# Linear attention stage of an adaLN block: the turn of a finished chunk behind the next unit's products on TensorE

## The chip, the cores and the metric

The kernel runs on one core of a Trainium2 chip. The metric is the device time of one execution in microseconds. Before the change the median of three runs is 692.49 us (689.46 to 693.12).

## What is computed

The reference is one block with adaptive layer norms over `x` of 8 batches, 512 tokens and 128 features: a causal linear attention, then a softmax attention and a mixture of experts. The part around the change is the linear attention:

```python
q = (jax.nn.elu(q) + 1.0 + FEAT_EPS) / jnp.sqrt(E)          # 16 heads of 8
k = jax.nn.elu(k) + 1.0 + FEAT_EPS
kv_cumsum = jnp.cumsum(jnp.einsum('blhe,blhf->blhef', k, v), axis=1)
k_cumsum = jnp.cumsum(k, axis=1)
num = jnp.einsum('blhe,blhef->blhf', q, kv_cumsum)
den = jnp.einsum('blhe,blhe->blh', q, k_cumsum)[..., None] + FEAT_EPS
out = (num / den).reshape(B, L, D) @ Wout.T + bout
```

Around it, in the same block: `x = x + ga * layernorm(out)`, `h = layernorm(x) * (1 + cb) + sb`, then queries, keys and values of the softmax attention from `h`, softmax attention over 512 tokens in 16 heads, and an expert per token (8 experts, 128 to 512 to 128, gelu).

## The kernel before, in words

The kernel is written engine by engine: each engine has its own program, and semaphores tie them together. In the linear stage all of them walk the same double loop, steps `s` from -3 to 8 (a pass for each batch) and in each `d` from 0 to 7. Unit `g = 8 s + d` is half of a chunk of 128 tokens of batch `s`: 8 of the 16 heads. A chunk `q` is two units.

What happens to a unit and a chunk:

- `products(g)` (TensorE, L912 to L925): eight matmuls of keys by queries into two banks, `b_at`. It waits until VectorE has masked unit g - 1 (`s_am`), since there is one pair of banks.
- `masked(g)` (VectorE, L1405 to L1410): two multiplications with the causal mask (L1409) from these banks into SBUF. It waits for the products (`s_at`) and for the numerators of unit g - 2 (`s_nm`).
- `numerators(g)` (TensorE, L927 to L940): sixteen recorded matmuls (L936) of masked products by values into bank `b_nm`. It waits for the mask and, in the first unit of a chunk, until ScalarE has copied the numerators of the chunk before.
- `numerators_out(q)` (ScalarE, L1956 to L1959): that copy, into `nt`.
- `turn(q)` (TensorE, L942 to L956): four transposes of `nt` (L946) and, for all chunks of a batch but the first, a matmul of the queries by the state of the earlier chunks (L952), into bank `b_tr`. It waits for the copy.
- `denominators(q)` and `normalise(q)` (VectorE, L1424 and L1429) divide. `turn_back(q)` (L961), `output_out(q)` (ScalarE, L1963), `project(q)` (L967) and `output(q)` (VectorE, L1437) make the output rows, and `squares(q)` (ScalarE, L2011) its squares.

Beside the units, the same steps carry the work of three other batches: the projections and features of batch s + 2 (`a_...`: L983, L990, L995, L1005, L1012 on TensorE; L1568, L1573, L1579, L1583 on VectorE; L1977, L1985, L1990, L1997, L2001, L2005 on ScalarE), the state of batch s + 1 (L975, masked by L1416), and layer norms and softmax projections of batches s - 2 and s - 3 (`c_...`: L1021, L1026, L1033, L1040 on TensorE; L1441, L1448, L1450, L1589 on VectorE; L2018, L2027, L2042, L2046 on ScalarE; L656 to L687 on POOL, where `h_ready` is L681 and L683). SP stores the features of a batch to DRAM (L208) and reads them back as stacks in twelve DMAs (L221).

The order on TensorE around the change, in an even step `d` (L1268 to L1316): `turn_back` of an earlier chunk; a projection, transposes or the state where that step has one; `turn` of the chunk whose second unit is g - 1; `products(g + 1)`; `numerators(g)`. Each engine takes its instructions in its program's order.

Behind the linear stage come the softmax attention (row maxima L1051 and L1596, scores L1079, exponentials L2058, values L1090) and the experts (L1338, L1347).

Of the kernel before, what the change touches and what calls it, by code (L numbers as in the profile page):

```python
# [199 lines left out]
def wait(eng, sem, value):  # L200

    if isinstance(value, int) and value <= 0:
        return
    eng.wait_ge(sem, value)
# [46 lines left out]
def program(nc, k):  # L251
# [21 lines left out]
    with ExitStack() as ctx, ExitStack() as early:  # L273
# [101 lines left out]
        def has(b):  # L375
            return 0 <= b < B

        def chunk(q):
            return 0 <= q < B * C

        def unit(g):
            return 0 <= g < B * NL
# [116 lines left out]
        with nc.Block() as block:  # L499
# [411 lines left out]
            def _(pe):  # L911
                def products(g):  # L912
                    b, d = g // NL, g % NL
                    c, hp, u = d // 2, d % 2, b % 2
                    if d == 0:
                        pe.wait_ge(k.s_stk[u], (b // 2 + 1) * N_STACK)
                    wait(pe, s_am, 2 * g)
                    for j in range(GH):
                        for gg in range(2):
                            p = GH * (2 * hp + gg) + j  # L920
                            rows = slice(HALF * LIN_HALF[p], HALF * LIN_HALF[p] + KR)
                            last = pe.matmul(b_at[gg][:, j * P:(j + 1) * P],  # L922
                                             ks[u][rows, LIN_SLOT[p], c * P:(c + 1) * P],
                                             qs[u][rows, LIN_SLOT[p], c * P:(c + 1) * P], start=True, stop=True)
                    last.then_inc(s_at, 1)  # L925
# [32 lines left out]
                def turn_back(q):  # L958
                    pe.wait_ge(s_on, q + 1)
                    wait(pe, s_yc, q)  # L960
                    pe.transpose(b_oy[:, 0:P], on[:, q % 2, :], k.ident).then_inc(s_ot, 1)  # L961

                def project(q):
                    if q == 0:
                        pe.wait_ge(w_s_v, SETUP)
                    pe.wait_ge(s_oc, q + 1)
                    pe.matmul(b_oy[:, 0:P], ot[:, q % 2, :], k.woutt[:], start=True, stop=True).then_inc(s_y, 1)  # L967

                def state(b):
                    pe.wait_ge(s_vp, b + 1)  # L970
                    pe.wait_ge(a_s_kc, b + 1)
                    wait(pe, c_s_r1, 2 * (b - 4) + 2)
                    for c in range(C - 1):
                        for i in range(c + 1):
                            last = pe.matmul(b_z[:, c * H * (E + 1):(c + 1) * H * (E + 1)], tile(k.h_all, b, i),  # L975
                                             vp[b % 2][:, i], start=(i == 0), stop=(i == c))
                    last.then_inc(s_sm, 1)

                def a_turn(a):
                    pe.wait_ge(a_s_xn, a + 1)  # L980
                    wait(pe, c_s_r1, 2 * (a - 5) + 1)
                    for c in range(C):
                        last = pe.transpose(b_x[:, c * P:(c + 1) * P], a_xn[:, c * D:(c + 1) * D], k.ident)  # L983
                    last.then_inc(a_s_tr, 1)

                def a_query(a):
                    pe.wait_ge(a_s_ht, a + 1)
                    if a == 0:
                        pe.wait_ge(w_s_v, QUERY)
                    pe.matmul(b_x[:], k.wlt[:, 0:D], a_ht[:], start=True, stop=True).then_inc(a_s_pj, 1)  # L990

                def a_key(a):
                    wait(pe, a_s_kc, a)
                    wait(pe, c_s_vc, a - 4)
                    pe.matmul(b_y[:], k.wlt[:, D:2 * D], a_ht[:], start=True, stop=True).then_inc(a_s_pj, 1)  # L995
# [13 lines left out]
                def a_key_turn(a):  # L1009
                    pe.wait_ge(a_s_ph, 2 * a + 2)  # L1010
                    for c in range(C):
                        last = pe.transpose(b_y[:, c * P:(c + 1) * P], a_fk[:, c * P:(c + 1) * P], k.ident)  # L1012
                    last.then_inc(a_s_kt, 1)
# [10 lines left out]
                def c_query(b):  # L1024
                    pe.wait_ge(c_s_ht, b + 1)
                    pe.matmul(b_x[:], k.wsm[:, 0:D], c_ht[:], start=True, stop=True).then_inc(c_s_pj, 1)  # L1026

                def c_key(b):
                    if has(b + 4):
                        pe.wait_ge(a_s_vc, b + 5)  # L1030
                    pe.wait_ge(s_sp, min(b + 4, B))
                    wait(pe, c_s_r1, 2 * b)
                    pe.matmul(b_z[:], k.wsm[:, D:2 * D], c_ht[:], start=True, stop=True).then_inc(c_s_pj, 1)  # L1033

                def c_value(b):
                    if has(b + 4):
                        pe.wait_ge(a_s_kc, b + 5)
                    wait(pe, c_s_vc, b)
                    for c in range(C):
                        last = pe.matmul(b_y[:, c * P:(c + 1) * P], c_ht[:, c * P:(c + 1) * P], k.wsm[:, 2 * D:3 * D],  # L1040
                                         start=True, stop=True)
                    last.then_inc(c_s_v, 1)
# [225 lines left out]
                for s in STEPS:  # L1268
                    for d in range(NL):
                        g = s * NL + d  # L1270
                        if s == -2 and d == 2:
                            pe.wait_ge(w_s_b, 16 * 5)
                            pe.transpose(k.bank[4][:, 0:P], wl_raw[:, 2, :], k.ident).then_inc(w_s_t, 1)
                        if s == -2 and d == 5:
                            pe.matmul(k.bank[3][0:B, :], ct, wm[:, 2 * D:NM * D], start=True, stop=True
                                      ).then_inc(w_s_m, 1)
                        if s == -1 and d == 5:
                            pe.wait_ge(w_s_v, WO)
                            pe.wait_ge(w_s_ct, 1)
                            pe.matmul(k.bank[4][:, P:2 * P], wo_pos, center, start=True, stop=True).then_inc(w_s_t, 1)  # L1280
                        if s == -1 and d == NL - 1:
                            pe.wait_ge(w_s_mr, 5)
                            pe.wait_ge(s_init, 1)
                        if d % 2 == 0 and chunk((g - 4) // 2):
                            turn_back((g - 4) // 2)
                        if d % 2 == 1 and chunk((g - 5) // 2):
                            project((g - 5) // 2)
                        if d == 0 and has(s - 3):
                            c_key(s - 3)
                        if d == 1 and has(s - 3):  # L1290
                            c_value(s - 3)
                        if d == 1 and has(s + 2):
                            a_turn(s + 2)
                        if d == 2 and has(s + 1) and s != -1:
                            state(s + 1)
                        if d == 3 and has(s + 2):
                            a_query(s + 2)
                            a_key(s + 2)
                        if d == 4 and has(s + 2):
                            a_value(s + 2)  # L1300
                        if d == 5 and has(s - 2):
                            c_turn(s - 2)
                        if d == 7 and has(s + 2) and s != -1:
                            a_key_turn(s + 2)
                        if s == 0 and d == 0:
                            pe.wait_ge(a_s_vc, 2)
                            state(0)
                            a_key_turn(1)
                        if d == 7 and has(s - 2) and s < B:
                            c_query(s - 2)  # L1310
                        if d % 2 == 0 and chunk((g - 2) // 2):
                            turn((g - 2) // 2)
                        if unit(g + 1):
                            products(g + 1)
                        if unit(g):
                            numerators(g)  # L1316
                        if s == B:
                            for m in range(4 * d, 4 * d + 4):
                                early_maximum(m)
                            if d == 4:  # L1320
                                pe.wait_ge(s_nt, B * C)
                                turn_maxima(0, b_num)
# [957 lines left out]
```

## Time and profile before

| | |
|---|---|
| median of three runs | 692.49 us |
| lowest, highest | 689.46, 693.12 us |
| the profiled execution | 689.38 us |
| its span in the profile | 687.6 us |
| TensorE, VectorE, ScalarE, POOL busy | 89%, 86%, 73%, 60% |
| linear stage with products of units | 29 to 215 us |

The profile is of one execution. The span is the time from the first to the last recorded instruction, and the execution's own time holds 1.8 us more around it. A row of the timeline has its start, its length, the engine, the line, what is written and read, and in brackets how long the engine waited before it and who released it. The granted clock of TensorE is given as a share of 2.4 GHz.

### The profile page before, as it was taken

The numbers are of one execution on the slowest core, as the hardware profiler recorded it, in microseconds if no ns is written. First come the engines' busy times: TensorE is split into PE (matmuls) and PEld (weight loads), VectorE is DVE, ScalarE is ACT, GpSimd is POOL, SyncE is SP. The second block draws the span as 40 slices with busy tenths as digits, with TensorE's granted clock in tenths as the row PEclk, the third lists the DMA queues.
The fourth block names the chain that finished last, engine by engine and source line by source line (L and its number), as shares of the span: only waits on it lengthen the run. The fifth ranks groups of instructions, "written<-read, shape, count | busy, mean of one in ns | idle before, by whom it ended". The sixth has DMA issues, their size and how long they took to land.

```text
span 687.6 us, 16368 instructions
## 1 busy us (share of the span) xinstructions
PE 610.6 (89%) x5305; PEld 304.8 (44%) x5305; DVE 590.7 (86%) x1489; ACT 500.5 (73%) x1071; POOL 411.6 (60%) x922
## 2 busy tenths in 40 slices
PE   4689789988877788999999999999999999899994
PEld 2456456655544222222333332333323322589993
DVE  6878999998877988899999999999999994775552
ACT  3545677787655387888888888888888889765661
POOL 4213558667656642436676887877877862566553
PEclk9899999999999699999999999999999999999997
DMA  6564234335364121137110301203012010556510
GB/s 181 161 229 131 66 107 135 120 116 185 113 165 139 48 92 47 47 107 231 49 47 2 116 25 53 77 13 116 25 52 78 13 48 23 139 174 174 167 33 9
DMA packets 42899, 66.25 MB, mean 96 GB/s; under 512 B 7948, under 2 KB 36335, under 8 KB 39808
## 3 DMA queue, kind: packets, MB, share of 16 engines
q1 hardware_dynamic: 39232, 56.73, 27.9%
q0 software_dynamic: 3296, 8.41, 3.4%
q8 instruction: 44, 0.72, 0.4%
q14 instruction: 39, 0.32, 0.2%
q10 hardware_dynamic: 288, 0.07, 0.0%
HBM read 41.64 MB, written 22.26 MB: 93 GB/s over the span
## 4 chain that ended last, share of the span: by engine, by line
PE 53%; ACT 18%; DVE 16%; issue 6%; SPq 2%; POOL 2%; DMA 2%; ACTq 0%; POOLq 0%; DVEq 0%
PE bank L1090 12%; ACT arena L2058 11%; PE pair L1079 8%; PE bank L1051 7%; PE pair L1338 4%; DVE arena L1409 4%; DVE arena L1596 3%; PE bank L1101 2%; PE bank L1347 2%; PE pair L1347 2%; PE bank L936 2%; PE pair L1131 2%; DVE fq_all L1573 1%; PE pair L990 1%; PE pair L1051 1%
## 5 line engine op out<-in xcount | busy, mean ns | idle before, releaser
L2058 ACT ACTIVATE arena<-pair 128x512 f32<-128x512 f32 x506 | 278.1, 602 | 52.8 <-PE pair L1079 50.9
L1596 DVE TENSOR_REDUCE arena<-bank 128x1 f32<-128x512 f32 x388 | 251.3, 682 | 10.1 <-PE bank L1051 7.2
L1079 PE MATMUL pair<-q_stack,k_stack 64*128 64x512 bf16 x506 | 158.7, 388 | 5.4 <-ACT arena L2058 4.9
L1051 PE MATMUL bank<-k_stack,q_stack 63*128 63x512 bf16 x388 | 136.0, 394 | 10.3 <-DVE arena L1596 6.0
L1090 PE MATMUL bank<-arena,values 128*9 128x512 f32 x1024 | 134.7, 598 | 1.6 <-ACT arena L2058 1.5
L1409 DVE TENSOR_TENSOR arena<-bank,cst 128x512 f32<-128x512 f32 x128 | 82.0, 681 | 12.8 <-PE bank L922 12.5
L1596 DVE TENSOR_REDUCE arena<-pair 128x1 f32<-128x512 f32 x124 | 84.3, 680 | 2.7 <-PE pair L1051 2.3
L726 POOL TENSOR_TENSOR arena<-arena 128x32 f32<-128x32 f32 (+6 forms) x312 | 68.4, 219 | 24.4
L1051 PEld LDWEIGHTS bank<-k_stack,q_stack 63*128 63x128 bf16 x388 | 33.1, 93 | 110.5 <-ACT arena L2063 25.9
L1079 PEld LDWEIGHTS pair<-q_stack,k_stack 64*128 64x128 bf16 x506 | 40.7, 93 | 47.4 <-ACT arena L2058 23.2
L1051 PE MATMUL pair<-k_stack,q_stack 63*128 63x512 bf16 x124 | 48.8, 393 | 0.7 <-ACT v_all L2083 0.3
L1959 ACT ACTIVATE arena<-bank,den_eps 128x512 f32<-128x512 f32 x32 | 21.8, 680 | 33.9 <-PE bank L936 33.9
L890 POOL DMA_INDIRECT out_dram<-arena,e_token_u x32 | 31.2, 975 | 23.1 <-DVE arena L1904 19.6
L762 POOL DMA_INDIRECT token_rows<-arena,d_places_u x32 | 33.6, 1050 | 15.4 <-POOL d_places_u L750 5.0
L2196 ACT ACTIVATE fq_all<-pair 128x512 f32<-128x512 f32 x39 | 23.3, 596 | 26.3 <-PE pair L1338 26.3
L1338 PE MATMUL pair<-q_stack,h_all 128*128 128x128 f32 x312 | 41.5, 276 | 0.0
L936 PE MATMUL bank<-arena,values 128*9 128x128 f32 x1024 | 40.4, 276 | 0.0
L649 POOL TENSOR_TENSOR arena<-arena 128x512 bf16<-128x512 f32 x15 | 17.4, 1161 | 35.5 <-ACT arena L2001 35.5
L1338 PEld LDWEIGHTS pair<-q_stack,h_all 128*128 128x128 f32 x312 | 38.0, 192 | 0.0
L922 PE MATMUL bank<-q_stack,k_stack 63*128 63x128 bf16 x512 | 25.6, 220 | 12.3 <-DVE arena L1409 11.2
L1090 PEld LDWEIGHTS bank<-arena,values 128*9 128x9 f32 x1024 | 15.2, 88 | 40.8 <-issue 29.9
L946 PE MATMUL bank<-cst,arena 128*128 128x128 f32 x128 | 20.4, 282 | 9.9 <-ACT arena L1959 9.7
(307 smaller groups left out, 1211.9 us busy)
## 6 DMA issues: line engine op xcount, KB each, us to landing
softmax_parts<-arena SPq DMA_DIRECT2D x8, 768.0 KB
q_stack<-softmax_parts SPq DMA_DIRECT2D x48, 128.0 KB
k_stack<-softmax_parts SPq DMA_DIRECT2D x48, 128.0 KB
linear_parts<-arena SPq DMA_DIRECT2D x7, 768.0 KB, 3.7
q_stack<-linear_parts SPq DMA_DIRECT2D x42, 128.0 KB
k_stack<-linear_parts SPq DMA_DIRECT2D x42, 128.0 KB
arena<-in_L_ffn_w_dram SPq DMA_DIRECT2D x16, 256.0 KB, 5.0
v_all<-token_rows SPq DMA_DIRECT2D x20, 192.5 KB, 2.7
```

Source lines behind the costliest of these rows:

```text
L726: done(pool.tensor_tensor(half[:, 0:w], src[:, 0:w], src[:, w:2 * w], ALU.add))
L762: pool.indirect_dma_start(k.rows_dram, bass.IndirectOffsetOnAxis(ap=k.pos_u[:, f:f + 1], axis=0), row_slot(f), None, bounds_check=NE * REG ...
L890: pool.indirect_dma_start(out_rows, bass.IndirectOffsetOnAxis(ap=token_u[:, j:j + 1], axis=0), yo[j], None, bounds_check=T * P - 1, oob_is ...
L936: last = pe.matmul(b_nm[VW * j:VW * j + E + 1, cols], vp[u][:, c, GH * (2 * hp + gg) + j, :], b_am[:, g % 2, gg, j, :], start=True, stop=T ...
L1051: pe.matmul(bank[:], qs[b % 2][rows, slot, qt * P:(qt + 1) * P], ks[b % 2][rows, slot, :], start=True, stop=True).then_inc(d_s_m, 1)
L1079: pe.matmul(score_bank(s)[:], ks[u][rows, 2 * g + x, kt * P:(kt + 1) * P], qs[u][rows, 2 * g + x, :], start=True, stop=True).then_inc(d_s_ ...
L1090: last = pe.matmul(b_num[VW * q:VW * q + E + 1, :], vp[b % 2][:, kt, GH * g + q, :], pt[:, kt % 2, q % 2, q // 2, :], start=(kt == 0), sto ...
L1338: last = pe.matmul(b_up[j % 2][:, c * P:(c + 1) * P], w1c[j % R4][:, c * P:(c + 1) * P], xt[j % R4], start=True, stop=True)
L1347: last = pe.matmul(b_dn[j % 2][:, 0:D], hid[j % R4][:, c * P:(c + 1) * P], k.w2_all[:, bass.ds(e * HID + c * D, D)], start=(c == 0), stop= ...
L1409: dve.tensor_tensor(b_am[:, g % 2, gg], k.tiles(b_at[gg][:], GH), k.rep(k.causal, GH), ALU.mult).then_inc(s_am, 1)
L1596: dve.reduce_max(mx[:, m % 2, col:col + 1], bank[:], AX).then_inc(d_s_mr, 1)
L2058: act.activation(pt[:, kt % 2, x, half, :], score_bank(s)[:], ACT.Exp, scale=SCALE).then_inc(d_s_e, 1)
```

## The change

In every even step the call of `turn` moves behind `products(g + 1)` and stands ahead of `numerators(g)`.

```diff
                         if d == 7 and has(s - 2) and s < B:
                             c_query(s - 2)
+                        if unit(g + 1):
+                            products(g + 1)
                         if d % 2 == 0 and chunk((g - 2) // 2):
                             turn((g - 2) // 2)
-                        if unit(g + 1):
-                            products(g + 1)
                         if unit(g):
                             numerators(g)
```

TensorE's program, pass s = 3, step 6 and the first half of step 7; behind each row are the semaphores that it waits for. Before:

```order
L961 MATMUL pair<-cst,arena 128x128 [waits b_projected_out,b_normalised]
L946 MATMUL bank<-cst,arena 128x128 [waits b_normalised,b_numerators_out]
L946 MATMUL bank<-cst,arena 128x128 x3
L952 MATMUL bank<-arena,fq_all 128x16x9
L922 MATMUL bank<-q_stack,k_stack 128x128 [waits b_masked]
L922 MATMUL bank<-q_stack,k_stack 128x128 x7
L936 MATMUL bank<-arena,values 9x128 [waits b_masked,b_numerators_out]
L936 MATMUL bank<-arena,values 9x128 x7
L967 MATMUL pair<-woutt,arena 128x128 [waits b_output_copied]
L1012 MATMUL pair<-cst,arena 128x128 [waits a_features]
L1012 MATMUL pair<-cst,arena 128x128 x3
L1026 MATMUL pair<-arena,wsm 128x512 [waits c_h_transposed]
```

After:

```order
L961 MATMUL pair<-cst,arena 128x128 [waits b_projected_out,b_normalised]
L922 MATMUL bank<-q_stack,k_stack 128x128 [waits b_masked]
L922 MATMUL bank<-q_stack,k_stack 128x128 x7
L946 MATMUL bank<-cst,arena 128x128 [waits b_normalised,b_numerators_out]
L946 MATMUL bank<-cst,arena 128x128 x3
L952 MATMUL bank<-arena,fq_all 128x16x9
L936 MATMUL bank<-arena,values 9x128 [waits b_masked,b_numerators_out]
L936 MATMUL bank<-arena,values 9x128 x7
L967 MATMUL pair<-woutt,arena 128x128 [waits b_output_copied]
L1012 MATMUL pair<-cst,arena 128x128 [waits a_features]
L1012 MATMUL pair<-cst,arena 128x128 x3
L1026 MATMUL pair<-arena,wsm 128x512 [waits c_h_transposed]
```

The five matmuls of the turn (L946, L952) now stand between the products (L922), which wait for the mask, and the numerators (L936).

The same engine in pass s = 7, step 2, where there is no projection beside the units, as one piece of the difference:

```order
 L961 MATMUL pair<-cst,arena 128x128
-L946 MATMUL bank<-cst,arena 128x128 x4
-L922 MATMUL bank<-q_stack,k_stack 128x128 x8
-L936 MATMUL bank<-arena,values 9x128 x8
-L967 MATMUL pair<-woutt,arena 128x128
-L922 MATMUL bank<-q_stack,k_stack 128x128 x8
-L936 MATMUL bank<-arena,values 9x128 x8
-L961 MATMUL pair<-cst,arena 128x128
-L946 MATMUL bank<-cst,arena 128x128 x4
```

This is the turn of a batch's first chunk: four transposes and no L952. In the difference it goes behind the first eight L922, and the next one, in step 4, goes behind the eight L922 that follow it. The orders of VectorE, ScalarE, POOL and SP are the same before and after.

## Rows read from the trace of the kernel before

**Rows 1.** The page, busy times; granted clock in 40 slices of 17.2 us.

```profile
PE 610.6 (89%) x5305; PEld 304.8 (44%) x5305; DVE 590.7 (86%) x1489; ACT 500.5 (73%) x1071; POOL 411.6 (60%) x922
...
PEclk9899999999999699999999999999999999999997
```

**Rows 2.** Stretches, whole core: length, busy us of each engine, clock, DMA.

```profile
110.00:134.00 24.00, 21.31 (x279) 14.31 (x276) 22.74 (x71) 18.55 (x49) 16.61 (x22) 1.00 0.43 133
...
182.00:222.00 40.00, 30.16 (x406) 18.75 (x405) 30.61 (x99) 22.50 (x62) 24.33 (x30) 1.00 0.56 159
```

**Rows 3.** Waits, 30 to 225 us: who waited for whom, us, times, longest.

```profile
DVE arena L1409 <- PE bank L922: 12.5, 15, 1.6
...
PE bank L922 <- DVE arena L1409: 11.2, 14, 2.0
...
PE bank L946 <- ACT arena L1959: 9.7, 16, 1.3
```

**Rows 4.** Timeline of TensorE, steps 6, 7 and 0 of a steady pass.

```profile
95.42 0.65 PE L946 MATMUL bank<-cst,arena 128*128 128x128 f32 x4 [0.55 <-ACT arena L1959]
...
97.33 0.40 PE L922 MATMUL bank<-q_stack,k_stack 63*128 63x128 bf16 x8 [1.01 <-DVE arena L1409]
...
97.66 0.62 PE L936 MATMUL bank<-arena,values 128*9 128x128 f32 x16
...
99.93 0.40 PE L922 MATMUL bank<-q_stack,k_stack 63*128 63x128 bf16 x8
...
102.27 0.65 PE L946 MATMUL bank<-cst,arena 128*128 128x128 f32 x4 [0.27 <-ACT arena L1959]
...
103.43 0.63 PE L936 MATMUL bank<-arena,values 128*9 128x128 f32 x16
```

**Rows 5.** Timeline of VectorE, the mask of the next pass.

```profile
100.86 1.27 DVE L1409 TENSOR_TENSOR arena<-bank,cst 128x512 f32<-128x512 f32 x2
```

**Rows 6.** Timeline of TensorE, ScalarE and VectorE, steps 2 to 4.

```profile
106.79 1.64 PE L975 MATMUL pair<-values,h_all 128*128 128x144 f32 x12
...
108.49 0.66 PE L946 MATMUL bank<-cst,arena 128*128 128x128 f32 x4
...
113.12 0.69 ACT L1959 ACTIVATE arena<-bank,den_eps 128x512 f32<-128x512 f32 x1 [2.56 <-PE bank L936]
...
114.88 0.75 DVE L1568 TENSOR_SCALAR fq_all<-pair,bq 128x512 f32<-128x512 f32 x1 [1.05 <-ACT arena L1990]
```

**Rows 7.** Timeline of VectorE and TensorE, passes 1 and 2 of the stage.

```profile
55.40 1.27 DVE L1409 TENSOR_TENSOR arena<-bank,cst 128x512 f32<-128x512 f32 x2
...
56.28 0.66 PE L946 MATMUL bank<-cst,arena 128*128 128x128 f32 x4 [0.55 <-ACT arena L1959]
...
71.52 0.66 PE L946 MATMUL bank<-cst,arena 128*128 128x128 f32 x4 [0.55 <-ACT arena L1959]
...
74.40 0.40 PE L922 MATMUL bank<-q_stack,k_stack 63*128 63x128 bf16 x8 [1.98 <-DVE arena L1409]
```

**Rows 8.** Timeline of ScalarE, behind the last store of the chain.

```profile
195.45 0.60 ACT L2042 ACTIVATE arena<-pair 128x512 bf16<-128x512 f32 x1 [4.16 <-DMA softmax_parts<-arena]
```

**Rows 9.** Timeline of POOL, VectorE and TensorE, the stage's last pass.

```profile
202.05 1.28 POOL L683 TENSOR_TENSOR h_all<-arena 128x512 f32<-128x512 f32 x1
...
202.79 1.29 DVE L1409 TENSOR_TENSOR arena<-bank,cst 128x512 f32<-128x512 f32 x2 [1.25 <-PE bank L922]
...
211.74 0.66 PE L946 MATMUL bank<-cst,arena 128*128 128x128 f32 x4 [0.88 <-ACT arena L1959]
```

**Rows 10.** Clock of one stretch; TensorE around two falls.

```profile
35.00:40.00 5.00, 4.85 (x43) 3.79 (x44) 3.17 (x14) 2.97 (x6) 2.43 (x4) 0.66 0.82 330
...
35.15 0.97 PE L983 MATMUL pair<-cst,arena 128*128 128x128 f32 x4 [1.84 <-ACT arena L1977]
...
36.05 0.61 PE L922 MATMUL bank<-q_stack,k_stack 63*128 63x128 bf16 x8
...
228.14 1.21 PE L1051 MATMUL bank<-k_stack,q_stack 63*128 63x512 bf16 x2 [1.80 <-DVE arena L1596]
```

## The prediction

> **What bounds the kernel now.** The page's busy shares [rows 1] name no single engine: TensorE 89%, VectorE 86%. So I went to the stage that the change touches, the linear stage, and read it by stretches [rows 2]: in a steady pass of 24 us VectorE is busy for 22.74 us and TensorE for 21.31, at full clock; in the last passes of the stage (182 to 222 us) VectorE is busy for only 30.61 of 40 us. The list of waits of the stage [rows 3] shows both sides of the exchange that is edited: the turn (L946) waits for ScalarE's copy of the numerators (L1959), 9.7 us in 16 waits; the products (L922) wait for VectorE's mask (L1409), 11.2 us in 14; and the mask waits for the products, 12.5 us in 15. (The PEld rows are weight loads of the same waits, and are not added.)
>
> **What the change does to one even step.** 31 turns are moved; the last one has no products behind it. Each even unit g has three ready times: P, when TensorE has ended what stands ahead; A, when ScalarE has copied the numerators (the turn needs it); M, when VectorE has masked unit g (the products of g+1 need it, since they overwrite the banks that were masked). The turn takes 0.84 us with its second matmul after a wait (0.78 when TensorE comes busy, 0.6 for the first chunk of a batch, which has no second matmul), the products take 0.33 (together 102.27 to 103.43 [rows 4]).
> Before: products at max(max(P, A) + 0.84, M), numerators 0.33 later.
> After: products at max(P, M), numerators at max(products + 0.33, A) + 0.84.
> So where the copy (A) comes last, the products win up to 0.84 us plus the wait and the numerators up to 0.33; where the mask (M) comes last, the turn no longer fills that wait, and the numerators and all behind them on TensorE lose up to 0.84. No instruction, semaphore or DMA is added; the orders of the other engines and of SP are the same. The consumer of the turn, VectorE's reciprocal (L1424), stands behind the mask of g+1, whose 1.28 us begin about 0.44 after the products; the turn is done by then, so its own delay costs nothing.
>
> **Steady pass, step 6 (M last).** Before, TensorE waited 0.55 us for A, the turn ran at 95.42 and the products waited for the mask until 97.33 [rows 4]. After, products still at 97.33, then the turn, numerators at 98.44 in place of 97.66: +0.78. Step 7 is dense (L967, L1012, L1026 back to back), so the products for unit 0 of the next pass go from 99.93 to 100.71, and their mask from 100.86 [rows 5] to 100.71 + 0.44 = 101.15: **+0.29**. In step 0 A (102.27) no longer costs anything, so TensorE is 0.39 late behind it. In step 2 L975 starts at 106.79 and takes about 1.47 to the next matmul, so P = 108.26, and A = 108.49 [rows 6]; before, numerators at 108.49 + 0.59 + 0.33 = 109.41; after, P = 108.65, A = 108.78 (it hangs on VectorE, +0.29), numerators at 109.54: +0.13. From there the chain runs over L990, L995 and the numerators of step 3 to ScalarE, which has waited 2.56 us for them [rows 6], and by the exp to VectorE's L1568, which has waited 1.05 us [rows 6]. VectorE's own 0.2 or 0.3 is absorbed in that 1.05, so a steady pass costs **+0.13**. The pattern stands in three passes (steps 2 at 108, 132 and 156 us): +0.39.
>
> **The first passes.** In the first, at 56.28, the turn waited for A, but M is 55.40 + 1.28 + 0.06 = 56.74 [rows 7]: after, numerators at 56.74 + 0.33 + 0.84 = 57.91 against 57.45, of which I keep **+0.42** (the turn comes without its wait) down to the exp of that pass. In the pass behind it the turn (71.52) stood inside the wait for M that ends at 74.40 [rows 7]; its 0.84 lands ahead of another wait for the mask, in step 7, so that pass and the next cost about 0.
>
> **The end of the stage.** The slip reaches the store of the last batch's parts. From there the chain is transfers and SP's issues until ScalarE goes on at 195.45, after 4.16 us of waiting for a store [rows 8]; TensorE's order doesn't matter in between. The store hangs on VectorE's step 0 and 1, +0.29. So 0.42 + 0.39 + 0.29 = **+1.1** arrive at 195.45. Behind it the change pays: VectorE waited 1.25 us, to 202.79, for products that stood behind a turn that waited for A [rows 9]. After, this mask starts at 201.6; the statistics behind it need POOL's h_all, which ends at 202.05 + 1.28 = 203.33, so they gain 0.76 of the 1.2. Over POOL's power chain and ScalarE this comes to the turn of 211.74 [rows 9], where A is now 210.98. M is the mask that is 0.7 earlier too (210.73), so the products go at 210.73, the turn at 211.06 and the numerators at 211.87 (0.03 of lag), in place of 211.74 + 0.84 + 0.33 = 212.91: **-1.03**, carried by L1026 and the last turn to VectorE's maxima. Sum of the plain terms: +1.1 - 1.03 = **+0.1 us**. Each term is uncertain by a few tenths (semaphore lags of 0.04 to 0.07), the sum by about 1.
>
> **The clock.** What the sum leaves out is that waits are no longer broken up. In a steady pass TensorE waited 0.55 us ahead of 95.42 and 1.01 ahead of 97.33 [rows 4]; after, it waits from 94.87 to 97.33, 2.5 us in one piece, in four passes; in the pass before from 70.97 to 74.40, 3.4 us in place of 0.55 and 1.98 [rows 7]. The granted clock shows what such waits did in this run [rows 10]: with 1.84 us of waiting ahead of 35.15 it fell from 2.4 to 1.2 GHz, and so it did with the 1.80 ahead of 228.14, behind a stretch with many short waits (the slice of 223 to 241 us has a mean between six and seven tenths [rows 1]); the 1.98 us ahead of 74.40 [rows 7], with the turn shortly before, did not bring it down (all slices from 52 to 223 us show 9 [rows 1]). So the cases lie near each other, and 2.5 or 3.4 us unbroken are beyond any that passed. Price of one fall: the stretch 35 to 40 us has a mean clock of 0.66 [rows 10], which is 3.4 of its 5 us at half speed; eight products that start at 36.05 took 0.61 there, first start to last end, against 0.40 at full clock, where the next group starts 0.33 behind (0.54 there), so 3.4 x (1 - 0.33/0.54) = 1.3 us of TensorE's work is lost, on a stretch (steps 7 and 0) whose 0.49 us of slack the 0.78 has already used. Bounds: 0 falls, 0 us; five falls, 6.6 us. I take two, nearest to what the mixed rows say: **+2.6**. The Trainium skill's page "TensorE: Matmul & The Clock Gate", section "HAM oscillation — how this bites in real kernels", says that a kernel whose matmuls wait in every round can fall back to the lower clock in every round. By that rule alone it would be all five. Our rows have waits on both sides, so it is a rival below and not the sum.
>
> Sum: +0.1 + 2.6 = +2.7 us against the profiled execution (689.38, span 687.6). The same on the median, 692.49, which lies 3.1 above that execution: **695.2 us**. A measurement of this kernel can tell about 0.5%, 3.5 us, from no change.
>
> **Rivals.**
> 1. The clock holds in all passes: +0.1, **692.6**. For it: 1.98 us ahead of 74.40 passed. Against: 1.80 and 1.84 did not.
> 2. It falls in all five waits, once in each: 5 x 1.3 + 0.1 = +6.6, **699.1**. For it: each wait is longer than any that passed. Against: with waits of 1.80 to 1.98 us the rows show both outcomes, so length alone does not decide.
> 3. Faster: the slips are swallowed (VectorE's idle 1.05 and the SP chain) and only the end gains, -1.0; and, since the stage ends denser, the low clock behind 223 us [rows 1] stays out. Rows 1 have about 0.35 of 17.2 us, 6 us, lost by the clock there, of which I take 2.3 on the chain (the rest lies beside VectorE's maxima): -3.3, **689.2**. The point from which it decides is whether TensorE waits less than now ahead of 228.14; that wait is for VectorE's statistics, which the change does not touch. Little speaks for it.
> 4. The turn is so late that VectorE's reciprocal waits for it, as at half clock (turn about 1.4 us, mask 1.28): some 0.3 in each of the 31 steps at worst, 9 us, but only at half clock; it widens rival 2, to about 700.
>
> **Chances.** Forecast (one to three falls, 694 to 697.5) 0.46, clock holds 0.24, all five or more 0.20, faster end 0.10. Of the forecast a bit over half lies within 0.5% (below 695.95): same 0.26 + 0.24 + 0.03 = 0.53; slower 0.20 + 0.20 = 0.40; faster than 689.03 by rival 3: 0.07. The range leaves out the ends of rivals 2, 3 and 4: 690.5 to 699.5.
>
> **What would show it.** In the changed kernel's profile: one wait of about 2.5 us ahead of the products in step 6 of each steady pass and none left ahead of the turn; VectorE's wait of 1.25 us ahead of the mask at 202.79 gone; granted clock below 1.00 in one to three slices between 70 and 180 us. No fall there, and the forecast's 2.6 is wrong. If the turn still waits for ScalarE in most steps, the reading of who comes last is wrong. If the stage ends earlier than before by more than 1 us at full clock, the steady slips are not on the chain.

## The result and the profile after

The changed kernel takes 702.72 us in the median of four runs (700.01 to 704.02) against 692.50 before (689.46 to 693.12): ratio 1.0149, 95% interval 1.0121 to 1.0177, or 10.2 us more. The forecast was 695.2, the range ended at 699.5. The profiled execution took 703.78 us, its span 702.0. The two profiled executions lie further apart than the medians, by 14.40 us: that of before, 689.38, is 3.1 us below its median, that of the changed kernel 1.1 above. Sums read from the traces answer to the 14.40, the ratio to the 10.2.

The page of the changed kernel, to be laid beside [rows 1] (a slice is now 17.55 us):

```profile
PE 627.8 (89%) x5305; PEld 315.9 (45%) x5305; DVE 592.0 (84%) x1489; ACT 501.8 (71%) x1071; POOL 411.5 (59%) x922
...
PEclk9888999889899769999999999999999999999998
```

VectorE, ScalarE and POOL have what they had; TensorE has 17.2 us more busy time for the same 5305 matmuls, and where [rows 1] has nines from 52 to 223 us, there are now four eights from 52 to 194 us (a slice with 3.4 us at half clock still has a mean of 0.90 and prints as a nine). The same stretches as [rows 2]:

```profile
110.00:134.00 24.00, 20.88 (x242) 14.23 (x243) 19.86 (x58) 16.14 (x40) 16.38 (x20) 0.86 0.43 133
...
182.00:222.00 40.00, 34.12 (x432) 21.91 (x431) 30.54 (x98) 22.41 (x60) 21.23 (x25) 0.89 0.44 120
```

In 110 to 134 us VectorE, the busiest engine there before (22.74 us in 71 instructions), does 19.86 in 58, at a mean clock of 0.86: less work gets through in the same 24 us. The waits that answer to [rows 3], for 30 to 235 us:

```profile
PE bank L922 <- DVE arena L1409: 21.8, 16, 3.4
...
PE bank L946 <- ACT arena L1959: 1.2, 2, 1.0
```

The turn hardly waits for ScalarE any more (1.2 us for 9.7), and the products wait twice as long for the mask (21.8 for 11.2). The change did what it says: it moved the wait and made one piece of two. TensorE around step 6 of the pass that [rows 4] show:

```profile
98.40 0.33 PE L961 MATMUL pair<-cst,arena 128*128 128x128 f32 x1
101.18 0.40 PE L922 MATMUL bank<-q_stack,k_stack 63*128 63x128 bf16 x8 [2.46 <-DVE arena L1409]
101.51 0.73 PE L946 MATMUL bank<-cst,arena 128*128 128x128 f32 x4
102.03 0.69 PE L952 MATMUL bank<-arena,fq_all 128*128 128x144 f32 x2
102.65 1.04 PE L936 MATMUL bank<-arena,values 128*9 128x128 f32 x16
...
127.03 0.61 PE L922 MATMUL bank<-q_stack,k_stack 63*128 63x128 bf16 x8 [2.47 <-DVE arena L1409]
...
153.90 0.61 PE L922 MATMUL bank<-q_stack,k_stack 63*128 63x128 bf16 x8 [2.46 <-DVE arena L1409]
...
180.99 0.61 PE L922 MATMUL bank<-q_stack,k_stack 63*128 63x128 bf16 x8 [2.47 <-DVE arena L1409]
```

One wait of 2.46 us, and behind it the L952 take 0.69 us and the sixteen L936 1.04, in place of 0.41 and 0.62. Stretches of it (length, busy us of each engine, clock):

```profile
102.00:105.40 3.40, 3.40 (x27) 2.60 (x26) 2.63 (x7) 2.62 (x7) 1.16 (x1) 0.50 0.00 0
105.50:109.00 3.50, 3.50 (x41) 1.64 (x40) 2.42 (x8) 2.80 (x8) 0.00 (x0) 1.00 0.00 0
125.90:132.70 6.80, 5.67 (x38) 3.82 (x38) 4.72 (x10) 4.17 (x9) 2.17 (x2) 0.50 0.36 128
...
153.20:160.00 6.80, 6.10 (x38) 3.82 (x38) 4.30 (x10) 3.75 (x8) 1.73 (x2) 0.50 0.19 66
```

0.50 is 1.2 GHz, 1.00 is 2.4 GHz: 3.4 us at the lower level behind the first of these waits, 6.8 us each behind the next two. In the trace every one of the six passes 0 to 5 has such a stretch at its step 6: 50.8 to 57.6, 78.1 to 81.5, 102.0 to 105.4, 125.9 to 132.7, 153.2 to 160.0 and 180.5 to 187.3 us, and 201.0 to 204.4 another: 37.5 us in all, where the kernel before has none between 38.7 and 226.5. VectorE then waits for TensorE's next products:

```profile
106.62 1.29 DVE L1409 TENSOR_TENSOR arena<-bank,cst 128x512 f32<-128x512 f32 x2 [1.08 <-PE bank L922]
```

The products of step 6 start later than before by 0.69 us in pass 0 (52.51 against 51.82), by 2.93 in pass 1 (77.33 against 74.40), then by 3.85 (101.18 against 97.33), 5.77 (127.03 against 121.26), 8.72 and 11.90, and the first maxima of the softmax stage (L1051) by 14.62 (231.72 against 217.10). The whole execution is 14.40 longer. So all of it arises in the linear stage, pass by pass.

### The profile page after: what moved, and what is told of

The parts are those of the page before. It is cut to its first block, busy times and chain, and to the rows that moved or that the text cites. A ratio compares the mean times of both kernels' runs of the same rounds, so it can differ in the third digit from the quotient of the medians.

```text
span 702.0 us, 16368 instructions
## 1 busy us (share of the span) xinstructions
PE 627.8 (89%) x5305; PEld 315.9 (45%) x5305; DVE 592.0 (84%) x1489; ACT 501.8 (71%) x1071; POOL 411.5 (59%) x922
## 4 chain that ended last, share of the span: by engine, by line
PE 63%; ACT 16%; DVE 10%; issue 4%; SPq 2%; DMA 2%; POOL 1%; ACTq 0%; POOLq 0%; DVEq 0%
PE bank L1090 12%; ACT arena L2058 11%; PE pair L1079 7%; PE bank L1051 7%; PE pair L1338 5%; PE bank L936 3%; DVE arena L1596 3%; DVE arena L1409 3%; PE pair L1347 3%; PE bank L1347 3%; PE bank L1101 2%; PE bank L922 2%; PE bank L946 2%; PE pair L975 2%; PE pair L1131 1%
## 5 line engine op out<-in xcount | busy, mean ns | idle before, releaser
L1051 PE MATMUL bank<-k_stack,q_stack 63*128 63x512 bf16 x388 | 136.5, 396 | 8.8 <-DVE arena L1596 4.8
L1409 DVE TENSOR_TENSOR arena<-bank,cst 128x512 f32<-128x512 f32 x128 | 82.0, 682 | 15.0 <-PE bank L922 14.8
L1051 PEld LDWEIGHTS bank<-k_stack,q_stack 63*128 63x128 bf16 x388 | 33.1, 93 | 110.0 <-ACT arena L2063 24.8
L1051 PE MATMUL pair<-k_stack,q_stack 63*128 63x512 bf16 x124 | 49.0, 395 | 0.6 <-ACT v_all L2083 0.3
L1959 ACT ACTIVATE arena<-bank,den_eps 128x512 f32<-128x512 f32 x32 | 21.8, 682 | 36.0 <-PE bank L936 35.9
L922 PE MATMUL bank<-q_stack,k_stack 63*128 63x128 bf16 x512 | 27.0, 229 | 21.8 <-DVE arena L1409 21.8
L936 PE MATMUL bank<-arena,values 128*9 128x128 f32 x1024 | 42.9, 289 | 0.0
L922 PEld LDWEIGHTS bank<-q_stack,k_stack 63*128 63x128 bf16 x512 | 15.4, 99 | 44.4 <-DVE arena L1409 29.2
L660 POOL TENSOR_SCALAR arena<-arena 128x4 f32<-128x4 f32 x16 | 3.7, 229 | 53.2 <-DVE arena L1450 53.2
```

The source lines that it names most:

```text
L922: last = pe.matmul(b_at[gg][:, j * P:(j + 1) * P], ks[u][rows, LIN_SLOT[p], c * P:(c + 1) * P], qs[u][rows, LIN_SLOT[p], c * P:(c + 1) * P ...
L936: last = pe.matmul(b_nm[VW * j:VW * j + E + 1, cols], vp[u][:, c, GH * (2 * hp + gg) + j, :], b_am[:, g % 2, gg, j, :], start=True, stop=T ...
L1051: pe.matmul(bank[:], qs[b % 2][rows, slot, qt * P:(qt + 1) * P], ks[b % 2][rows, slot, :], start=True, stop=True).then_inc(d_s_m, 1)
L1409: dve.tensor_tensor(b_am[:, g % 2, gg], k.tiles(b_at[gg][:], GH), k.rep(k.causal, GH), ALU.mult).then_inc(s_am, 1)
```

## The experiments

**Theory.** The wait in one piece of step 6 brings the clock down in every pass, and that is the loss. **First rival:** the order itself costs it (numerators and all behind them late, the turn late), and the lower clock only goes along with it. **Second rival:** the loss comes from the turns moved in the other steps. The kernels ran on other chips, in three groups (1 to 4; 5, 6, 9 and 10; 7, 8, 11 and 12), each with runs of the kernel before (medians 706.89, 706.37 and 706.02 us there), and are told by their ratio to it; 1% is 7.1 us. Times in the expectations of 1 to 4 are those of the first chip, so only their ratios can be compared. No trace of the kernel before was taken on those chips. Those chips need some 14 us more for the kernel before. It lies behind the linear stage (in experiment 1 L1051 starts 2.62 us later than in the trace of before, and the execution ends 17.0 later) and was not followed up. Times of the trace are compared with the trace of before shown above. Lines behind an edit are numbered a few higher in these kernels (L1409 is L1412 or L1415 there, L975 is L976).

**1. The wait filled.** Changed order, but in step 6 of passes 0 to 5 the turn is also issued ahead of the products, without its signal; the real one, behind, writes the same over it. So the order that counts is the changed one, with 0.84 us of matmuls in the wait.

```diff
+                        if d == 6 and 0 <= s < 6:
+                            turn((g - 2) // 2, False)
                         if unit(g + 1):
                             products(g + 1)
```

> The changed order; in step 6 of passes 0 to 5 the five matmuls of the turn are also issued ahead of the products (their result is written over by the real turn behind the products, so nothing is left out). TensorE's wait for the mask is broken up as before, and the delay of 0.78 us of the numerators stays. Clock theory (the fall to 1.2 GHz behind the unbroken wait costs the time): no low clock between 45 and 210 us, time 691 to 694 us, 9 to 11 us under the changed kernel. Rival, the order itself (each pass's numerators, ScalarE and POOL come later): 700 to 703 us, with the clock at 2.4 GHz.

Measured: 706.98 us, ratio 1.0011 (0.9994 to 1.0028). The lower clock is left at 75.5 to 79.0 and 123.3 to 126.7 us, 6.8 us in all. With five more matmuls per pass nearly all of the loss is gone, so the order by itself isn't what costs 1.5%: the first rival falls as the explanation. What the order does cost is measured in 5. The expectation of no lower clock at all was missed by two passes of six.

**2. One step put back.** Changed order, but in step 6 up to pass 5 the turn stands ahead again.

```diff
+                        ahead = d == 6 and s < 6
+                        if chunk_ready and ahead:
+                            turn((g - 2) // 2)
                         if unit(g + 1):
                             products(g + 1)
-                        if chunk_ready:
+                        if chunk_ready and not ahead:
                             turn((g - 2) // 2)
```

(`chunk_ready` stands for `d % 2 == 0 and chunk((g - 2) // 2)`. The next experiments have the same form, and only `ahead` is shown.)

> The changed order, but in step 6 of passes up to 5 the turn stands ahead of the products again; 25 of 31 turns stay moved. Clock theory: no low clock in the steady passes, and the gain at the end of the stage (about 1.9 us between unit 56 and unit 63 in the changed kernel's trace) stays: 690 to 691.5 us. Rival, each moved turn costs a little: about 10.2 x 25/31 = 8 us over the kernel before, 700 us.

Measured: 705.24 us, ratio 0.9976 (0.9955 to 0.9998). The turns moved elsewhere cost nothing in sum: the second rival falls. But the trace is not free of the lower clock, as it was expected to be: it has 17.1 us of it, at 54.9 to 58.3, 75.3 to 78.7, 123.1 to 126.5, 188.0 to 191.4 and 208.5 to 211.9 us. The third of these lies in a steady pass, behind a wait that was broken up:

```profile
122.33 0.40 PE L922 MATMUL bank<-q_stack,k_stack 63*128 63x128 bf16 x8 [1.12 <-DVE arena L1412]
```

```profile
123.10:126.50 3.40, 3.40 (x16) 1.78 (x8) 2.83 (x7) 3.06 (x7) 1.16 (x1) 0.50 0.11 33
```

**3. That step alone.** The order of before, moved in step 6 of passes 0 to 5 alone, six turns of 31.

```diff
+                        ahead = not (d == 6 and 0 <= s < 6)
```

> The kernel before, with the turn moved only in step 6 of passes 0 to 5 (6 of 31). Clock theory: all of the loss and none of the gain at the end: 10.2 + 1.9 = 12 us over the kernel before, 703 to 706 us, with a low clock in each of the six passes. Rival, each moved turn costs a little: 10.2 x 6/31 = 2 us, 694.5 us.

Measured: 718.33 us, ratio 1.0158 (1.0141 to 1.0175), 34.1 us of lower clock between 45 and 225 us, L1051 at 231.12. Two of its waits:

```profile
100.69 0.40 PE L922 MATMUL bank<-q_stack,k_stack 63*128 63x128 bf16 x8 [2.46 <-DVE arena L1412]
...
126.54 0.61 PE L922 MATMUL bank<-q_stack,k_stack 63*128 63x128 bf16 x8 [2.46 <-DVE arena L1412]
```

The six turns give the whole loss, and the second wait shows the products (0.61 us) already at the lower clock.

**4. The last passes alone.** The order of before, moved in passes 6 to 8 alone.

```diff
+                        ahead = s < 6
```

> The kernel before, with the turn moved only in passes 6 to 8. If the gain of the stage's end is the products that no longer stand behind a turn that waits for ScalarE: 1 to 2 us faster than before, 690.5 to 691.5 us, first maxima (L1051) 1 to 2 us earlier, clock as before up to 222 us. Rival, in the changed kernel the end only caught up because its chain of stores had slack: no difference, 692.5 us.

Measured: 706.06 us, ratio 0.9981 (0.9960 to 1.0002). The interval reaches 1, so a gain is not shown, and its trace has none: in the last passes the clock falls at 188.4 to 191.8 and 208.9 to 212.3 us, which was not expected, and the kernel is 2.41 us behind the trace of before at step 6 of pass 5 and 2.96 behind at L1051. The second of these falls begins with step 4 of pass 7, where the mask comes last and the turn no longer stands ahead of the products:

```profile
207.74 0.30 PE L961 MATMUL pair<-cst,arena 128*128 128x128 f32 x1 [0.98 <-DVE v_all L1440]
208.84 0.61 PE L922 MATMUL bank<-q_stack,k_stack 63*128 63x128 bf16 x8 [0.81 <-DVE arena L1412]
```

Of the seven traces with this order in step 4 of the last passes (the changed kernel's two, 1, 2, 4, 6, 7), five have such a fall between 188 and 225 us (all but 1 and 7), 3.4 to 6.8 us in all; the three that keep the turn ahead there (9, 11, 12) have none up to 223 us.

**5. That step, with the wait filled.** As 3, with the copy of 1: the price of the order without most of the clock's.

```diff
+                        if d == 6 and 0 <= s < 6:
+                            turn((g - 2) // 2, False)
+                        ahead = not (d == 6 and 0 <= s < 6)
```

> Turn moved only in step 6 of passes 0 to 5, and there its five matmuls are also issued ahead of the products (written over by the real turn): the delay of the numerators by itself, at full clock, without the gain of the other turns. By the sum of the prediction +1.1 us over the kernel before (ratio 1.0016); by the offsets of the run in which the turn is issued twice (+0.37 in a pass without low clock) 6 x 0.37 = +2.2 us, ratio 1.003. Rival, the delay costs its whole 0.78 in every pass: +4.7 us, ratio 1.007.

Measured: 709.61 us, ratio 1.0039 (1.0015 to 1.0064), 2.8 us. TensorE in step 6:

```profile
122.18 0.66 PE L946 MATMUL bank<-cst,arena 128*128 128x128 f32 x4 [0.55 <-ACT arena L1965]
122.68 0.41 PE L952 MATMUL bank<-arena,fq_all 128*128 128x144 f32 x2
124.10 0.40 PE L922 MATMUL bank<-q_stack,k_stack 63*128 63x128 bf16 x8 [1.01 <-DVE arena L1415]
124.42 0.66 PE L946 MATMUL bank<-cst,arena 128*128 128x128 f32 x4
```

Its products of step 6 come at 99.80, 124.10, 148.40 and 172.69 us, that is 2.47, 2.84, 3.22 and 3.60 behind those of before: 0.37 a pass at full clock. Falls of 3.4 us are left in passes 0 and 1 (52.2 and 76.1 us).

3 and 5 have the same order and differ in the copy alone: 1.0158 against 1.0039. This pair weighs most for the theory.

**6. Less in the wait.** Changed order, with only one matmul of the turn (a transpose) in the wait of step 6, at the same place as the copy of 1.

```diff
+                        if d == 6 and 0 <= s < 6:
+                            pe.wait_ge(s_nt, (g - 2) // 2 + 1)
+                            wait(pe, s_on, (g - 2) // 2)
+                            pe.matmul(b_tr[:, 0:P], nt[:, (g - 2) // 2 % 2, 0:P], k.ident, start=True, stop=True,
+                                      is_transpose=True, skip_group_check=True)
```

> The changed kernel, with one matmul of the turn (of five, 0.27 us) issued in the wait of step 6 of passes 0 to 5 (written over later). If any break in the wait holds the clock: as with the whole turn, ratio 1.001. If it is the amount of work in the wait: the clock still falls in most passes, ratio 1.010 to 1.015. Rival of no clock effect at all: 1.015.

Measured: 713.36 us, ratio 1.0086 (1.0057 to 1.0115), 20.5 us of lower clock. It stands in the trace (the transpose takes 0.33 us, not the 0.27 expected) as

```profile
124.33 0.33 PE L1314 MATMUL bank<-cst,arena 128*128 128x128 f32 x1 [0.55 <-ACT arena L1964]
126.24 0.40 PE L922 MATMUL bank<-q_stack,k_stack 63*128 63x128 bf16 x8 [1.58 <-DVE arena L1414]
```

and 1.58 us unbroken behind it. This pass holds. Of the six step-6 waits four still have a fall behind them, of 3.4 us each (13.7 us; the rest of the 20.5 lies in the last passes): less filling, less gain. So neither of the two clear-cut expectations came true; 1.0086 lies between them.

**7. The same work elsewhere.** A control for 1: changed order, the copy in step 4 in place of step 6.

```diff
+                        if d == 4 and 0 <= s < 6:
+                            turn((g - 2) // 2, False)
```

> Control: the changed kernel, the second copy of the turn's five matmuls put into step 4 of passes 0 to 5, where TensorE has no wait ahead of the products, in place of step 6 (written over as before). Clock theory: the wait of 2.5 us in step 6 is whole, the clock falls as in the changed kernel: ratio 1.013 to 1.018. Rival, any additional work of TensorE in a pass holds the clock: ratio 1.001 as with the copy in step 6.

**8. The changed kernel, once more,** in the same group as 7.

> The changed kernel again, on the chip of these runs: ratio 1.012 to 1.018 as before if the loss is that of the kernel and not of the first chip.

Measured: the control 714.28 us, ratio 1.0106 (1.0066 to 1.0146), 30.7 us of lower clock; the changed kernel 716.98 us, ratio 1.0135 (1.0094 to 1.0177), 41.0 us. A step 6 of the control, then a stretch around two step 6 there:

```profile
100.69 0.40 PE L922 MATMUL bank<-q_stack,k_stack 63*128 63x128 bf16 x8 [2.46 <-DVE arena L1412]
101.02 0.66 PE L946 MATMUL bank<-cst,arena 128*128 128x128 f32 x4
101.52 0.42 PE L952 MATMUL bank<-arena,fq_all 128*128 128x144 f32 x2
101.86 1.04 PE L936 MATMUL bank<-arena,values 128*9 128x128 f32 x16
```

```profile
98.00:106.00 8.00, 5.54 (x47) 3.40 (x47) 6.29 (x12) 5.89 (x14) 3.58 (x3) 0.79 0.21 68
122.00:132.00 10.00, 7.54 (x69) 5.05 (x69) 8.07 (x17) 7.10 (x18) 5.24 (x5) 0.68 0.47 143
```

The same stretches of 5, with the same order in step 6 and the wait filled:

```profile
98.00:106.00 8.00, 6.99 (x81) 4.56 (x83) 7.72 (x18) 6.96 (x19) 2.70 (x3) 1.00 0.17 44
122.00:132.00 10.00, 8.81 (x109) 6.05 (x110) 9.69 (x26) 8.18 (x21) 3.77 (x5) 1.00 0.26 91
```

The copy in step 4 leaves the wait of 2.46 us and the falls behind it; most of the loss stays. The control came out below what was expected of it, but its interval overlaps that of the changed kernel, so whether it helps at all is not settled.

The executions of one kernel, whose order is the same in all, say the same. Time and mean granted clock of the fastest and the slowest: the control 707.92 us at 0.955 and 716.37 at 0.941, experiment 6 706.65 at 0.961 and 714.88 at 0.946, the changed kernel 712.18 at 0.952 and 719.15 at 0.939. That is 7 to 8.5 us for some 20 us more at half clock, 0.36 to 0.41 us for each.

**9 to 12. Looking for a better order.** First (9) the order that the traces suggest: the turn ahead where the mask comes last (step 6 up to pass 5, step 4 of the last passes), behind elsewhere, and the copy in the step 6 named.

```diff
+                        if d == 6 and 0 <= s < 6:
+                            turn((g - 2) // 2, False)
+                        ahead = (d == 6 and s < 6) or (d == 4 and s >= 6)
```

> Turn ahead of the products where the mask comes last (step 6 of passes up to 5, step 4 of passes 6 and 7), behind them elsewhere; in step 6 of passes 0 to 5 it is issued twice, both ahead of the products. If the low clock in the kernel before's own waits (a wait of 1.98 us in pass 1) costs something, the second copy takes it away: ratio 0.994 to 0.996, 3 to 4 us. If the second copy does nothing, the ratio is that of the run with step 6 ahead, 0.9976.

Measured: 704.87 us, ratio 0.9988 (0.9964 to 1.0012): no gain is shown; the interval holds the 0.9976 expected if the copy did nothing, and not the 0.994 to 0.996. Then (10) the order of before with the turn twice in step 6 of passes 0 to 5, both ahead of the products (`ahead = True`, and the copy as above):

> The kernel before, with the turn issued twice in step 6 of passes 0 to 5, both ahead of the products (no order changed). If the clock of the kernel before also falls in some executions in these waits (it did in two profiled runs of this series, at 55 to 62 and 75 to 79 us): 1 to 2 us faster, ratio 0.997 to 0.9985. Rival, TensorE is on the path there and 0.8 us more work costs: ratio 1.002 or more.

Measured: 704.34 us, ratio 0.9975 (0.9957 to 0.9994). Then (11) both gains: this order and copy up to pass 5, and from pass 6 the turn behind the products but in step 4.

```diff
+                        if d == 6 and 0 <= s < 6:
+                            turn((g - 2) // 2, False)
+                        ahead = s < 6 or d == 4
```

> Both parts that were faster: the order of the kernel before up to pass 5 with the turn issued twice in step 6, and the turn behind the products in passes 6 to 8 but for step 4, where the mask comes last. If the two gains add up (0.9975 and 0.9981): ratio 0.9955 to 0.996, 3 us. If both are the same executions' gain: 0.9975.

Measured: 702.46 us, ratio 0.9963 (0.9942 to 0.9984), the lowest of these medians and between the two cases of the expectation. The page's clock line and one of the filled waits:

```profile
PEclk9899999999998599999999999999999999978998
```

```profile
96.20 0.60 PE L946 MATMUL bank<-cst,arena 128*128 128x128 f32 x4
96.64 0.41 PE L952 MATMUL bank<-arena,fq_all 128*128 128x144 f32 x2
97.38 0.40 PE L922 MATMUL bank<-q_stack,k_stack 63*128 63x128 bf16 x8 [0.33 <-DVE arena L1415]
```

Its stage runs to pass 5 as before does (97.38 for 97.33), and L1051 starts at 215.96, 1.14 earlier. Last (12), with a third turn in the wait of passes 0 and 1 (`for copy in range(2 if s < 2 else 1)` around the copy):

> As the run before it, and in passes 0 and 1, whose waits are longest (0.89 and 1.98 us behind the turn), the turn is issued three times. If the low clock that the runs still show near 55 and 75 us costs 1 to 2 us: ratio 0.993 to 0.995. If TensorE's slack there is already used: ratio 0.996 to 0.998.

Measured: 703.32 us, ratio 0.9960 (0.9943 to 0.9977), which the interval doesn't tell from the one before it.

## Why the prediction was wrong, and where right

**Who comes last: right.** The waits came as written: about 2.5 us forecast in step 6 of the steady passes, 2.46 found; 3.4 in pass 1, 3.42 found; the turn's wait for the copy is gone but for 1.2 us.

**The end of the stage: right in this trace, the closeness in part luck.** -1.03 forecast. ScalarE goes on 15.63 us late (211.08 against 195.45; it is released by L1033 now and no longer by the store), and the first maxima are 14.62 late: -1.01. From the first products of pass 7 it is -1.05 (15.67 behind), and 1, 7, 9, 11 and 12 have -0.7 to -1.1 there. But 3, 5 and 10, whose last passes have the order of before, have -0.2 to -0.4 as well, and in 2, 4, 6 and 8, with a fall in pass 7, nothing is left of it (-0.1 to +0.2). The forecast had left those falls out. ScalarE after the change:

```profile
211.08 0.60 ACT L2042 ACTIVATE arena<-pair 128x512 bf16<-128x512 f32 x1 [4.09 <-PE pair L1033]
```

The mask of [rows 9], 202.79 before, was to start at 201.6; in the timeline of VectorE after the change it is

```profile
217.23 1.29 DVE L1409 TENSOR_TENSOR arena<-bank,cst 128x512 f32<-128x512 f32 x2 [0.50 <-PE bank L922]
```

and 217.23 less the 15.67 us that the stage is late there is 201.56. Of its wait of 1.25 us, which I had called gone, 0.50 is left.

**The plain slips: under-sized.** +0.13 a steady pass was forecast, 0.37 is measured (5), so +1.1 for the slips should have been about 2.2, if passes 0 and 1, which had falls in 5 too, slip like the others. The step at fault is that for step 2: I took 1.47 us from L975 to the next matmul, experiment 1 shows 1.56, and the turn behind the products takes 0.84 (124.42 to 125.26 in 5), not 0.78. I had read 0.23 us of slack where there was 0.14.

```profile
158.56 1.64 PE L976 MATMUL pair<-values,h_all 128*128 128x144 f32 x12
160.12 0.40 PE L922 MATMUL bank<-q_stack,k_stack 63*128 63x128 bf16 x8
```

With both put right the forecast's own sum for step 2 gives about 0.3. Its 109.54 is 0.03 short of its own terms too (108.65 + 0.33 + 0.59 = 109.57). What is missing to 0.37 stays open.

**The clock: the step that failed.** "I take two, nearest to what the mixed rows say: +2.6". There were falls in all six passes, pass 0 among them, which I had left out of the five. Its step 6 before, then after:

```profile
50.03 0.66 PE L946 MATMUL bank<-cst,arena 128*128 128x128 f32 x4 [0.55 <-ACT arena L1959]
51.82 0.40 PE L922 MATMUL bank<-q_stack,k_stack 63*128 63x128 bf16 x8 [0.89 <-DVE arena L1409]
```

```profile
52.51 0.61 PE L922 MATMUL bank<-q_stack,k_stack 63*128 63x128 bf16 x8 [2.34 <-DVE arena L1409]
```

And four of the six falls lasted 6.8 us, two 3.4, so that with the one at 201.0 us 37.5 us ran at the lower clock in place of 6.8. I had priced every fall at 3.4 us from the stretch of 35 to 40 us [rows 10], though the other fall that I named there, ahead of 228.14, lasts twice as long in the same trace:

```profile
226.50:233.30 6.80, 4.98 (x15) 1.50 (x15) 6.28 (x17) 3.84 (x12) 5.29 (x8) 0.50 0.02 5
```

The price of a microsecond was about right: up to the products of unit 6 of pass 6 (204.00) the slip is 15.86 us. Of it 0.69 stood there ahead of the first fall and 6 x 0.37 is the order's, which leaves 13.0, over 37.5 us 0.35 each; I had 1.3 / 3.4 = 0.38. Experiment 3 gives nearly the same by itself: 14.45 us at the end of pass 6, less 0.54 and 2.2, over 34.1 us, 0.34. Pass by pass it varies: 0.55 us for the fall of pass 1, 1.55 for that of pass 2, both of 3.4 us, 2.6 and 2.8 for those of 6.8 in passes 3 and 4. 0.7 + 13.0 + 2.2 - 1.05 is 14.8, against 14.62 at L1051 and 14.40 for the whole; that only puts the measured slip together again and is no second proof. So what failed is the term for the clock, by the number and the length of the falls; the next largest miss is the 1.1 of the slips.

Rival 2, falls in all waits, was the mechanism, with 0.20 where the forecast had 0.46; at one fall of 3.4 us per pass it still gave too little, 699.1. The rule of the Trainium skill's page "TensorE: Matmul & The Clock Gate", section "HAM oscillation — how this bites in real kernels", that a kernel which waits in every round can start every round at the lower clock, agrees with this trace, six passes of six; the page tells it of waits for DMAs, here they are waits for VectorE. I had set against it the 1.98 us of [rows 7] that passed. But that wait had the turn right ahead of it (71.52 to about 72.4), and this is what the change removes. And that it passed was one execution's luck: the same wait of 1.98 us, with the turn or its copy right ahead of it, has a fall with it in 1, 2 and 5 (from 75.5, 75.3 and 76.1 us), and none in 4. In the steady passes (2 to 5) of all traces, two waits with the turn between (0.55 and 1.0 to 1.1 us) went with full clock in 18 of 20 (before, 1, 2, 4, 5), with one transpose between in 2 of 4 (6), and one wait of 2.46 us in none of 16 (the changed kernel twice, 3, 7).

**How the low clock reaches VectorE.** At full clock the step-6 waits of before come every 23.92 us (97.33, 121.26, 145.18). In the changed kernel they come 26.87 and 27.09 us apart behind the falls of 6.8 us (127.03, 153.90, 180.99). The low clock makes products late, VectorE waits for them (1.08 us at 106.62), and its mask is late. The loss doesn't grow by this: the wait of step 6 stays 2.46 or 2.47 us, and each fall costs anew.

**When a fall is long.** The same single wait of 2.46 us has falls of 3.4 and of 6.8 us with it. They differ in when they begin. Of the 24 step-6 falls of the changed kernel (twice), 3 and 7, sixteen began while TensorE still waited (125.9, with the products at 127.03), and fifteen of these lasted 6.8 us, one 3.4 (180.3 in 7). Eight began behind the first products (102.0, with the products at 101.18), and all eight lasted 3.4. With shorter or broken waits this doesn't hold: in 2 a fall that began at 75.3 us, with the products at 75.60, lasted 3.4, and in 4 one that began at 55.3, with the products at 54.42, lasted 6.8.

**Left open.** Why a fall begins early in one wait and late in the next. Experiments 1 and 2 still had a fall at 123 us, behind the same broken waits that held in other passes. The gains of 2, 4, 9, 10, 11 and 12 lie within each other's intervals. That 2, 10, 11 and 12 beat before is shown, each by its own interval; that 11, the lowest of several tried, beats 2 or 10 is not. Whether 11 gains by its copies or by its end alone is not told apart either.

## What to carry over

Ahead of moving work behind a wait, ask what that work does inside the wait: here 0.84 us of matmuls that seemed to cost a delay of numerators kept two short waits from becoming one of 2.46 us, and such a wait in each of six passes cost about 13 us of the trace by the clock. Decide such an order step by step, by which operand comes last there, not for all steps alike: with step 6 put back the loss was gone (2), though over before such a choice gained only 0.2% to 0.4% in the medians of 2 and 11, and in 9 nothing that is shown. Don't rest on one execution in which a wait passed: take the same wait in several. Where a wait can't be broken up by work that is due, matmuls whose result is written over can stand in it: they brought 1.0149 down to 1.0011, and 1.0158 to 1.0039.

## What the runs showed that I had not expected

- Waits of 2.34 to 3.43 us on TensorE, between stretches that are busy but with gaps, came with the lower clock in all six passes, in the changed kernel (both traces) and in experiments 3 and 7.
- A fall lasts 3.4 us or 6.8 us here, not one length; with the single waits of step 6 all long ones began while TensorE still waited.
- In the last passes two waits of 0.9 and 0.8 us with one matmul (L961) between them had falls behind them in five of seven traces.
- One transpose in the wait (1 of 5 matmuls, experiment 6) took about half of the lower clock away: 20.5 us in place of 41.0 (8) or 37.5; five left 6.8. It is not all or nothing.
- Ending the stage 1.14 us earlier (11) did not remove the lower clock behind 223 us: the clock line shows a five and an eight there.
